# The beginning of a one-core attention and expert kernel: when the late weights are loaded, which projections TensorE makes first, and which engine rounds the first keys

## The chip, the core and the metric

The kernel runs on one core of a Trainium2 chip. A core has TensorE (PE in the profile; PEld is its weight load), VectorE (DVE), ScalarE (ACT), GpSimd (POOL) and SyncE (SP), each with a queue of its own that is worked off in order, and 16 DMA engines, to which SP and ACT give transfers here. The metric is the device time of one execution in microseconds (us), lower is better.

## What is computed

16 sequences of 512 rows of 128 numbers, in float32, go through an attention block with 16 heads of 8 columns, a layer norm, a layer of 8 experts of which each row takes 2, and another layer norm:

```python
x = _layernorm(x + _L0_attn_ref(x, Wq, bq, Wk, bk, Wv, bv, Wo, bo))     # (16, 512, 128)
# in it: scores = einsum('bhqd,bhkd->bhqk', Q, K) / sqrt(8); probs = softmax(scores)
#        intervened = probs without key 0, normalised again
#        combined = probs + 0.5 * (intervened - probs); attn_out = combined @ V, then @ Wo.T + bo
x = _layernorm(x + _L0_ffn_ref(x, gate_w, w1, w2, w3))                  # 8 experts, top 2, silu
```

## The kernel before

**Units.** The attention is cut into 64 units: a unit u is a sequence b = u // 4 and a group of 4 heads. A unit is taken through three stages in three consecutive periods. In period p the kernel makes the row maxima of unit p + 2, the scores and exponentials of unit p, and the sums over values of unit p - 1. A period has 8 steps k, and periods -2 and -1 come ahead of the first unit; they hold only maxima and preparation. `maxima(u, c)` (L632) is four bf16 matmuls into four banks `mx_ps` for the query block c of 128 rows; VectorE reduces the four banks in one instruction (L1016), and PE may write them again only then. So one block of maxima is made per two steps, and PE and DVE take turns on `mx_ps`.

**How float32 is kept.** Q and K are projected in float32 (`behind`, names q0, q1, k0, k1: query or key, first or second half of the sequence), copied to `full_q_sb`, `full_k_sb` by ACT with the bias (L855), and split into three bf16 parts. For sequence 0 DVE makes the split (`lead`, `rest`: first part, remainder, second part, remainder as third part), for the later ones POOL (`split_lead`, `split_rest`). The parts are stored to DRAM (`q_parts_d`, `k_parts_d`) and come back in the layout that the matmuls need: as operands of the maxima (`load_maxima(u)`, four loads of 64 KB: `QM`, `KM`, names `q_maxima_sb`, `k_maxima_sb`) and of the scores (`load_qk(u)`, two loads of 288 KB, `region_sb`).

**What stands at the beginning.** SP loads the first sequence's x (`xT_sb[0]`), Wk and the second x, and then, in eight issues, the weights that are not needed at once: Wv, the gate, Wo in four pieces, bv and bo. ACT loads Wq and the two biases, and waits for both biases before its first copy. PE runs 16 spare matmuls on a tile of ones, the four projections of sequence 0, and 96 more spare matmuls (`WARMING`), while the parts go to DRAM and come back. Then the periods start. In the periods -2 and -1, each block of maxima is followed by 8 spare matmuls of 512 columns (L724). The table `ONCE` says which other work stands at which step there: gc and gw fold the gate into Wv and Wo (gc waits for all eight late weights and for a halved Wo that ACT makes), v0 and v1 are the values of sequence 0, q0 to k1 with a 1 the projections of sequence 1. The projections of sequence 2 follow by the table `BEHIND`: q0 of sequence 2 at step 3 of period -1, k1 at step 3 of period 0.

**SP's queue behind that.** In this order: the stores of the first parts of sequence 0 (two for K), `load_maxima(0)` (its two Q loads are ACT's), `load_maxima(1)`, the stores of the other planes of K (three) and Q (one), `load_maxima(2)`, `load_qk(0)` and `load_qk(1)` (both wait for these stores), `load_xT(2)` (which waits until v1 of sequence 0 has been computed, since it overwrites `xT_sb[0]`), `load_qk(2)`, `load_qk(3)`, `move_negmax(0)` (the negated maxima of unit 0 as rows of the scores' operand; it waits for POOL's `split_negmax(0)`), and the stores of sequence 1.

**POOL** clears the value tiles, adds bv to the values (`values_with_bias(0)`, `values_without_key0(0)`), then splits Q of sequence 1. That split waits until the last store of Q's parts of sequence 0 has landed, as it writes the same tile.

## Time and profile before

| | us |
|---|---|
| median of 3 runs | 1178.43 (1175.75 to 1179.16) |
| the profiled execution, its own time | 1177.16 |
| its span, first to last instruction | 1175.0 |

| engine | busy us | share of the span |
|---|---|---|
| PE | 1116.9 | 95% |
| DVE | 927.2 | 79% |
| ACT | 824.8 | 70% |
| POOL | 663.2 | 56% |

The reductions of the maxima run from 17.7 to 742.7 us of the span; the experts and the last layer norm follow. The part that the change touches is the first 50 us. The granted clock of PE is 1.00 throughout. A row of the timeline gives the start in us from the span's start, the duration of the merged instructions, the engine, the line, the operation, what it writes and reads, how many there are, and in brackets the idle time ahead of it with what ended it. SPq and ACTq are the issues of DMAs on these queues: the duration is that of the issue, not of the transfer.

### The profile page before, as it was taken

The page shows a single profiled execution, that of the slowest core. Times are in us where ns is not written, and L with a number is a line of the kernel's source. Part 1 is how long each engine was busy: PE and PEld are TensorE (multiplying, and loading weights), DVE is VectorE, ACT ScalarE, POOL GpSimd, SP SyncE. Part 2 cuts the span into 40 slices and gives each one's busy share as a digit, 9 for nine tenths or more (in the row PEclk, how much of TensorE's full clock was granted, in tenths as well). Part 3 has the DMA queues.
Part 4 walks back from the last instruction along what each step waited for, and adds up shares of the span by engine and source line. Part 5 has one row for each costly group of instructions (what it writes and reads, how often), then busy time and mean ns, then how long its engine had stood idle before and what let it go on. Part 6 is the DMA issues. An engine that isn't in the chain of part 4 may idle for free. (4 is left out here: it accounts for less than half of the span.)

```text
span 1175.0 us, 23587 instructions
## 1 busy us (share of the span) xinstructions
PE 1116.9 (95%) x7236; PEld 575.7 (49%) x7240; DVE 927.2 (79%) x1421; ACT 824.8 (70%) x1668; POOL 663.2 (56%) x1003
## 2 busy tenths in 40 slices
PE   9999999999999999999999998999999999999986
PEld 6422232232222222222322222279999999999962
DVE  6888999999999999999999999855545554444435
ACT  2588888988889889888889888853544434345627
POOL 4424556666676676676676654666545433334336
PEclk9999999999999999999999999999999999999998
DMA  4453334444434343443443345353434333332247
GB/s 145 148 159 112 106 119 124 132 126 127 126 119 138 117 134 117 131 130 109 135 129 125 123 144 159 92 120 84 89 77 103 87 76 80 78 71 58 58 152 301
DMA packets 175051, 139.79 MB, mean 119 GB/s; under 512 B 89539, under 2 KB 151623, under 8 KB 174928
## 3 DMA queue, kind: packets, MB, share of 16 engines
q1 hardware_dynamic: 165672, 119.95, 36.3%
q0 software_dynamic: 8688, 18.14, 4.6%
q8 instruction: 60, 0.98, 0.4%
q14 instruction: 63, 0.52, 0.1%
q10 hardware_dynamic: 568, 0.20, 0.1%
HBM read 95.96 MB, written 42.19 MB: 118 GB/s over the span
## 5 line engine op out<-in xcount | busy, mean ns | idle before, releaser
L837 ACT ACTIVATE probs_sb<-ring_ps 128x512 f32<-128x512 f32 x1024 | 558.4, 598 | 96.9 <-PE ring_ps L643 81.1
L1016 DVE TENSOR_REDUCE rowmax_sb<-mx_ps 128x4 f32<-128x2048 f32 x256 | 586.0, 2289 | 26.3 <-PE mx_ps L632 20.7
L643 PE MATMUL ring_ps<-region_sb 74*128 74x512 bf16 x1024 | 311.4, 384 | 2.1 <-ACT probs_sb L837 2.0
L655 PE MATMUL acc_ps<-probs_sb,values_sb 128*32 128x512 f32 x2048 | 272.3, 604 | 0.0
L1690 POOL DMA_INDIRECT y_d<-probs_sb,values_sb x135 | 133.0, 985 | 190.0 <-DVE probs_sb L1329 166.0
L643 PEld LDWEIGHTS ring_ps<-region_sb 74*128 74x128 bf16 x1024 | 79.2, 97 | 312.8 <-ACT probs_sb L837 272.4
L912 ACT ACTIVATE xT_sb<-region_sb 128x512 f32 x78 | 49.2, 630 | 183.1 <-PE mx_ps L762 181.7
L1329 DVE SCALAR_TENSOR_TENSOR probs_sb<-ring_ps,values_sb 128x128 f32<-128x128 f32 x135 | 42.1, 347 | 143.2 <-issue 120.9
L1546 POOL DMA_INDIRECT rows_d<-sent_sb,pos_sb x128 | 130.1, 1016 | 41.2 <-issue 19.2
L632 PE MATMUL mx_ps<-k_maxima_sb,q_maxima_sb 32*128 32x512 bf16 x1024 | 101.0, 384 | 40.4 <-DVE rowmax_sb L1016 39.9
L783 PE MATMUL ring_ps<-region_sb,probs_sb 128*128 x1080 | 133.5, 275 | 1.6 <-DVE probs_sb L1339 1.6
L783 PEld LDWEIGHTS ring_ps<-region_sb,probs_sb 128*128 128x128 f32 x1080 | 131.0, 192 | 5.0 <-issue 2.2
L752 PE MATMUL mx_ps<-k_parts_sb,xT_sb 128*128 128x256 f32 (+1 forms) x624 | 130.5, 352 | 1.0 <-DVE k_parts_sb L1311 1.0
L1339 DVE TENSOR_TENSOR probs_sb<-mx_ps,probs_sb 128x512 f32<-128x512 f32 (+1 forms) x156 | 95.2, 619 | 25.9 <-PE mx_ps L762 18.6
L752 PEld LDWEIGHTS mx_ps<-k_parts_sb,xT_sb 128*128 128x128 f32 x624 | 106.8, 190 | 13.9 <-DVE k_parts_sb L1311 2.2
L655 PEld LDWEIGHTS acc_ps<-probs_sb,values_sb 128*32 128x32 f32 x2048 | 40.5, 108 | 97.9 <-issue 97.5
L632 PEld LDWEIGHTS mx_ps<-k_maxima_sb,q_maxima_sb 32*128 32x128 bf16 x1024 | 25.7, 90 | 111.7 <-DVE rowmax_sb L1016 102.8
L958 ACT ACTIVATE probs_sb<-mx_ps 128x1024 f32<-128x1024 f32 (+1 forms) x78 | 70.4, 903 | 4.5 <-PE mx_ps L752 4.4
L762 PE MATMUL mx_ps<-k_parts_sb,full_q_sb 128*128 128x256 f32 (+1 forms) x312 | 65.5, 353 | 0.0
L762 PE MATMUL mx_ps<-k_parts_sb,full_k_sb 128*128 128x256 f32 (+1 forms) x312 | 64.6, 350 | 0.0
L762 PEld LDWEIGHTS mx_ps<-k_parts_sb,full_q_sb 128*128 128x128 f32 x312 | 51.6, 191 | 5.3 <-issue 0.8
L1399 POOL CAST negmax_parts_sb<-negmax_sb 16x128 bf16<-16x128 f32 x64 | 17.9, 279 | 62.9 <-PE mx_ps L632 62.7
(193 smaller groups left out, 1174.6 us busy)
## 6 DMA issues: line engine op xcount, KB each, us to landing
region_sb<-q_parts_d SPq DMA_DIRECT2D x64, 288.0 KB
region_sb<-k_parts_d SPq DMA_DIRECT2D x64, 288.0 KB
k_parts_d<-k_parts_sb SPq DMA_DIRECT2D x46, 256.0 KB, 2.5
k_maxima_sb<-k_parts_d SPq DMA_DIRECT2D x128, 64.0 KB
probs_sb<-y_d SPq DMA_DIRECT2D x32, 256.0 KB, 6.9
q_maxima_sb<-q_parts_d SPq DMA_DIRECT2D x126, 64.0 KB
values_sb<-rows_d SPq DMA_DIRECT2D x57, 132.0 KB, 2.3
q_parts_d<-q_parts_sb SPq DMA_DIRECT2D x15, 384.0 KB
```

The lines of the kernel that those rows point to most:

```text
L632: last = nc.tensor.matmul(mx_ps[:, j, :], q[rows, P * c:P * (c + 1)], k[rows, :], start=True, stop=True)
L643: nc.tensor.matmul(bank, KS[b % 2][0:KR + MR, h, P * c:P * (c + 1)], QS[b % 2][0:KR + MR, h, :], start=True, stop=True).then_inc(s_ring_re ...
L655: last = nc.tensor.matmul(acc_ps[VW * j:VW * (j + 1), 0, :], VE[b % 2][:, c, HG * g + j, :], PT[u % 2][:, j, c, :], start=(c == 0), stop=( ...
L752: last = nc.tensor.matmul(up_ps[:, c, 0:n], W1T[t % 2][:, P * c:P * (c + 1)], XGT[t % 2][:, 0:n], start=True, stop=True)
L762: last = nc.tensor.matmul(lin_ps[:, c, 0:n], W3T[t % 2][:, P * c:P * (c + 1)], XGT[t % 2][:, 0:n], start=True, stop=True)
L783: last = nc.tensor.matmul(y_ps[:, at:at + D], HH[t % 2][:, c, P * w:P * (w + 1)], W2[:, bass.ds(expert + c * D, D)], start=(c == 0), stop= ...
L837: nc.scalar.activation(PT[u % 2][:, i // QC, i % QC, :], ring_bank("st", u, i), ACT.Exp, scale=SCALE).then_inc(s_ring_done, 1)
L958: nc.scalar.activation(SG[t % 2][:, :, 0:n], up_ps[:, :, 0:n], ACT.Silu).then_inc(s_silu, 1)
L1016: V.tensor_reduce(rowmax[u % 2][:, :].rearrange("p (j c) -> p j c", c=QC)[:, :, c], mx_ps[:, :, :], axis=AXX, op=ALU.max, negate=True).the ...
L1339: V.tensor_tensor(HH[t % 2][:, part, 0:n], lin_ps[:, part, 0:n], SG[t % 2][:, part, 0:n], ALU.mult)\
L1546: G.indirect_dma_start(rows_d, bass.IndirectOffsetOnAxis(ap=pos[b % 2][:, s, c:c + 1], axis=0), XE[b % 2][:, c, s, :], None).then_inc(s_sc ...
L1690: G.indirect_dma_start(y_d, bass.IndirectOffsetOnAxis(ap=XG[t % RING][:, w, D:D + 1].bitcast(i32), axis=0), YO[t % YRING][:, w, :], None, ...
```

## The change

Five things are edited: (1) PE's second block of spare matmuls has 80 instead of 96, and the 8 behind a block of maxima are 5 where the same or the next step holds an entry of `ONCE`; (2) the eight late loads stand on SP's queue behind `load_maxima(0)` instead of behind the second x; (3) `ONCE` has the projections of sequence 1 first, and gc, gw, v0, v1 after them, and POOL splits Q of sequence 1 ahead of its work on the values; (4) the first part of K of sequence 0 is rounded by ACT instead of DVE, so DVE's `lead(1)` begins with the remainder; (5) the biases have a semaphore each, so the copy of Q waits for bq alone.

```diff
-WARMING = (16, 96)
+WARMING = (16, 80)
...
-        s_biases_qk = sem("biases_qk")
+        s_biases_qk = [sem(f"bias_{n}") for n in "qk"]
+        s_first_cast = sem("first_keys_cast")
...
-        ONCE = {(-2, 1): ("gc", 0), (-2, 2): ("gw", 0), (-2, 3): ("v0", 0), (-2, 4): ("v1", 0), (-2, 5): ("q0", 1),
-                (-2, 6): ("q1", 1), (-2, 7): ("k0", 1), (-1, 0): ("k1", 1)}
+        ONCE = {(-2, 1): ("q0", 1), (-2, 2): ("q1", 1), (-2, 3): ("k0", 1), (-2, 4): ("k1", 1), (-2, 5): ("gc", 0),
+                (-2, 6): ("gw", 0), (-2, 7): ("v0", 0), (-1, 0): ("v1", 0)}
...
             load_xT(1)
-            for dst, src in ((wvg_sb[:, 0:D], wvT), (gate_sb[:, :], gateT)):
-                sp.dma_start(dst, src).then_inc(s_weights, 16)
...
-            sp.dma_start(bo_sb[:, :], bo.to_broadcast([P, D])).then_inc(s_weights, 16)
...
-            sp.wait_ge(s_first_split, 4)
+            sp.wait_ge(s_first_cast, 1)
             sp.dma_start(by_head(k_parts_d[0, 2:3]), qk_parts[1][:, 0:1, :]).then_inc(s_first_stored[1], 16)
-            sp.wait_ge(s_first_split, 6)
+            sp.wait_ge(s_first_split, 5)
             sp.dma_start(by_head(k_parts_d[0, 0:2]), qk_parts[1][:, 0:2, :]).then_inc(s_first_stored[1], 16)
             load_maxima(0)
+            for dst, src in ((wvg_sb[:, 0:D], wvT), (gate_sb[:, :], gateT)):
+                sp.dma_start(dst, src).then_inc(s_weights, 16)
...
+            sp.dma_start(bo_sb[:, :], bo.to_broadcast([P, D])).then_inc(s_weights, 16)
             load_maxima(1)
...
-                            for n in range(8):
+                            for n in range(5 if {(p, k), (p, k + 1)} & ONCE.keys() else 8):
                                 nc.tensor.matmul(acc_ps[:, 0, :], QM[p + 2][:, 0:P], KM[p + 2][:, :], start=True, stop=True)
...
-            act.wait_ge(s_biases_qk, 16 * 2)
...
+                    elif name[1] == "0":
+                        act.wait_ge(s_biases_qk[which], 16)
...
             for what in BEFORE:
                 behind(*what)
+            act.wait_ge(s_ring_done, ring_at["k1", 0] + 1)
+            nc.scalar.activation(qk_parts[1][:, 0, :], full[1][:, :], ACT.Copy).then_inc(s_first_cast, 1)
             act.wait_ge(*first_stored(0))
...
-                dve.wait_ge(s_ring_done, ring_at[("q1", "k1")[which], 0] + 1)
-                V.tensor_copy(parts[:, 0, :], exact[:, :]).then_inc(s_first_split, 1)
-                dve.wait_ge(s_first_split, n + 1)
+                if which == 0:
+                    dve.wait_ge(s_ring_done, ring_at["q1", 0] + 1)
+                    V.tensor_copy(parts[:, 0, :], exact[:, :]).then_inc(s_first_split, 1)
+                    dve.wait_ge(s_first_split, 1)
+                else:
+                    dve.wait_ge(s_first_cast, 1)
...
             clear(1)
+            split_lead(1, 0)
+            split_rest(1, 0)
             values_with_bias(0)
             values_without_key0(0)
-            split_lead(1, 0)
-            split_rest(1, 0)
             beside_reduction(-1, 1)
```

**PE, from the spare matmuls to the second block of unit 1, before.** `mx_ps` is written by a block of maxima, `acc_ps` by spare matmuls; `wq_sb`, `wk_sb` mark projections, `centre_sb` to `bo_sb` gc, `ysum_sb` gw, `wv_gate_sb,xT_sb` the values.

```order
L714 MATMUL acc_ps<-ones_sb 128x256 x96
L632 MATMUL mx_ps<-k_maxima_sb,q_maxima_sb 128x512 x4
L724 MATMUL acc_ps<-k_maxima_sb,q_maxima_sb 128x512 x8
L679 MATMUL ring_ps<-gate_sb,centre_sb 128x8
L680 MATMUL ring_ps<-ident_sb,wo_half_gate_sb 128x128
L681 MATMUL ring_ps<-ident_sb,bo_sb 128x128
L632 MATMUL mx_ps<-k_maxima_sb,q_maxima_sb 128x512 x4
L724 MATMUL acc_ps<-k_maxima_sb,q_maxima_sb 128x512 x8
L685 MATMUL ring_ps<-wv_gate_sb,ysum_sb 128x8 x2
L690 MATMUL ring_ps<-wv_gate_sb,xT_sb 128x136 x2
```

The same stretch of PE now, to gc and the block of maxima behind it:

```order
L715 MATMUL acc_ps<-ones_sb 128x256 x80
L633 MATMUL mx_ps<-k_maxima_sb,q_maxima_sb 128x512 x4
L725 MATMUL acc_ps<-k_maxima_sb,q_maxima_sb 128x512 x5
L674 MATMUL ring_ps<-xT_sb,wq_sb 128x256
L633 MATMUL mx_ps<-k_maxima_sb,q_maxima_sb 128x512 x4
...
L725 MATMUL acc_ps<-k_maxima_sb,q_maxima_sb 128x512 x5
L674 MATMUL ring_ps<-xT_sb,wk_sb 128x256
L680 MATMUL ring_ps<-gate_sb,centre_sb 128x8
L681 MATMUL ring_ps<-ident_sb,wo_half_gate_sb 128x128
L682 MATMUL ring_ps<-ident_sb,bo_sb 128x128
L633 MATMUL mx_ps<-k_maxima_sb,q_maxima_sb 128x512 x4
```

The group gc has moved from behind the first block of maxima to behind the third, where it follows the last projection of sequence 1; v1 now stands behind the first block of unit 1, in period -1.

**SP, from the second x on, now** (before, the rows of `wvT` to `bo` stood directly behind the second `xT`, ahead of the stores):

```order
L419 DMA xT_sb<-xT 128x512
L488 DMA q_parts_d<-q_parts_sb 128x2x512
L490 DMA k_parts_d<-k_parts_sb 128x512
L492 DMA k_parts_d<-k_parts_sb 128x2x512
L457 DMA k_maxima_sb<-k_parts_d 64x1x512 x2
L495 DMA wv_gate_sb<-wvT 128x128
L495 DMA gate_sb<-gateT 128x8
L497 DMA wo_sb<-woT 32x1x128 x4
L499 DMA bv_sb<-bv 128x128
L500 DMA bo_sb<-bo 128x128
L456 DMA q_maxima_sb<-q_parts_d 64x1x512
L457 DMA k_maxima_sb<-k_parts_d 64x1x512
```

The eight issues now stand ahead of `load_maxima(1)` and of all that follows it: the other stores, `load_maxima(2)`, `load_qk(0)`, `load_qk(1)` and `load_xT(2)`, whose order among themselves is as before.

## Rows read from the trace of the kernel before

**Rows 1.** The line L1016 alone: duration ns min/median/max, first and last start.

```profile
L1016 DVE TENSOR_REDUCE rowmax_sb<-mx_ps x256: 2256/2293/2296, 17.7 to 742.7; 128x4 f32<-128x2048 f32 x128
```

**Rows 2.** The timeline, start of the kernel to the first maxima.

```profile
5.58 0.84 ACT L855 ACTIVATE full_q_sb<-ring_ps,bq_sb 128x256 f32<-128x256 f32 x2 [1.86 <-DMA bk_sb<-bk]
6.36 0.95 ACT L855 ACTIVATE full_k_sb<-ring_ps,bk_sb 128x256 f32<-128x256 f32 x2
6.64 10.64 PE L714 MATMUL acc_ps<-ones_sb 128*128 128x256 bf16 x96
7.98 0.42 DVE L992 CAST k_parts_sb<-full_k_sb 128x512 bf16<-128x512 f32 x1
9.61 0.37 SPq L498 DMA_DIRECT2D k_parts_d<-k_parts_sb  x1
11.83 1.15 SPq L463 DMA_DIRECT2D k_maxima_sb<-k_parts_d  x2
17.21 0.10 PEld L632 LDWEIGHTS mx_ps<-k_maxima_sb,q_maxima_sb 32*128 32x128 bf16 x4 [0.21 <-issue]
```

**Rows 3.** The page: a group by line, with busy us, mean ns, idle before.

```profile
L912 ACT ACTIVATE xT_sb<-region_sb 128x512 f32 x78 | 49.2, 630 | 183.1 <-PE mx_ps L762 181.7
```

**Rows 4.** Busy time by stretch: PE, PEld, DVE, ACT, POOL, PEclk, DMA share, GB/s.

```profile
11.50:15.50 4.00, 4.00 (x39) 3.57 (x38) 3.47 (x1) 0.31 (x1) 3.78 (x5) 1.00 0.25 73
23.00:35.00 12.00, 11.67 (x68) 5.75 (x67) 9.17 (x4) 3.23 (x10) 7.55 (x11) 1.00 0.76 213
```

**Rows 5.** The timeline: reductions of the maxima, second, fifth and sixth block.

```profile
20.46 2.29 DVE L1016 TENSOR_REDUCE rowmax_sb<-mx_ps 128x4 f32<-128x2048 f32 x1 [0.51 <-PE mx_ps L632]
29.61 2.29 DVE L1016 TENSOR_REDUCE rowmax_sb<-mx_ps 128x4 f32<-128x2048 f32 x1 [0.73 <-PE mx_ps L632]
32.41 2.29 DVE L1016 TENSOR_REDUCE rowmax_sb<-mx_ps 128x4 f32<-128x2048 f32 x1 [0.51 <-PE mx_ps L632]
```

**Rows 6.** The timeline: gc and its halved Wo; one cycle of period -1.

```profile
12.00 0.31 ACT L849 ACTIVATE wo_half_gate_sb<-wo_sb 128x128 f32<-128x128 f32 x1 [4.69 <-issue]
19.07 0.41 PEld L679 LDWEIGHTS ring_ps<-gate_sb,centre_sb 128*128 128x128 f32 x2
19.56 0.27 PE L681 MATMUL ring_ps<-ident_sb,bo_sb 128*128 128x128 f32 x1
31.95 0.10 PEld L632 LDWEIGHTS mx_ps<-k_maxima_sb,q_maxima_sb 32*128 32x128 bf16 x4 [0.42 <-DVE rowmax_sb L1016]
32.29 1.90 PE L724 MATMUL acc_ps<-k_maxima_sb,q_maxima_sb 128*128 128x512 bf16 x8
33.81 0.41 PEld L673 LDWEIGHTS ring_ps<-xT_sb,wq_sb 128*128 128x128 f32 x2
34.66 0.47 ACT L855 ACTIVATE full_q_sb<-ring_ps,bq_sb 128x256 f32<-128x256 f32 x1 [2.18 <-PE ring_ps L673]
34.75 0.10 PEld L632 LDWEIGHTS mx_ps<-k_maxima_sb,q_maxima_sb 32*128 32x128 bf16 x4 [0.54 <-DVE rowmax_sb L1016]
```

**Rows 7.** The timeline: issues on SP's queue.

```profile
2.18 0.43 SPq L424 DMA_DIRECT2D wv_gate_sb<-wvT  x1
6.56 0.43 SPq L429 DMA_DIRECT2D bo_sb<-bo  x1
16.71 0.45 SPq L506 DMA_DIRECT2D q_parts_d<-q_parts_sb  x1
21.46 0.81 SPq L475 DMA_DIRECT2D region_sb<-q_parts_d  x1
25.80 0.34 SPq L418 DMA_DIRECT2D xT_sb<-xT  x1
```

**Rows 8.** Issues of one DMA each: count, KB, us from issue to landing.

```profile
q_parts_d<-q_parts_sb SPq DMA_DIRECT2D x1, 256.0 KB, 2.2
xT_sb<-xT SPq DMA_DIRECT2D x1, 256.0 KB, 5.6
```

**Rows 9.** The timeline: PE's first spare matmuls.

```profile
1.06 3.60 PE L710 MATMUL acc_ps<-ones_sb 128*128 128x256 bf16 x16 [1.06 <-POOL ones_sb L1371]
```

More of the change, by code:

```diff
@@ L380, in split_done @@
         def split_done(b, which):
-            return (s_first_split, 8 - which) if b == 0 else (s_split, split_no(b, which) + 1)
+            return (s_first_split, 7 - which) if b == 0 else (s_split, split_no(b, which) + 1)
         def halves(t):
@@ L422, in _ @@
             load_xT(1)
-            for dst, src in ((wvg_sb[:, 0:D], wvT), (gate_sb[:, :], gateT)):
-                sp.dma_start(dst, src).then_inc(s_weights, 16)
-            for j in range(HG):
-                sp.dma_start(wo_sb[VW * j:VW * (j + 1), :],
-                             woT.rearrange("(g j d) n -> j g d n", j=HG, d=DK)[j]).then_inc(s_weights, 16)
-            sp.dma_start(bv_sb[:, :], bv.to_broadcast([P, D])).then_inc(s_weights, 16)
-            sp.dma_start(bo_sb[:, :], bo.to_broadcast([P, D])).then_inc(s_weights, 16)
             def by_head(planes):
@@ L494, in _ @@
             sp.dma_start(by_head(q_parts_d[0, 0:2]), qk_parts[0][:, 0:2, :]).then_inc(s_first_stored[0], 16)
-            sp.wait_ge(s_first_split, 4)
+            sp.wait_ge(s_first_cast, 1)
             sp.dma_start(by_head(k_parts_d[0, 2:3]), qk_parts[1][:, 0:1, :]).then_inc(s_first_stored[1], 16)
-            sp.wait_ge(s_first_split, 6)
+            sp.wait_ge(s_first_split, 5)
             sp.dma_start(by_head(k_parts_d[0, 0:2]), qk_parts[1][:, 0:2, :]).then_inc(s_first_stored[1], 16)
             load_maxima(0)
+            for dst, src in ((wvg_sb[:, 0:D], wvT), (gate_sb[:, :], gateT)):
+                sp.dma_start(dst, src).then_inc(s_weights, 16)
+            for j in range(HG):
+                sp.dma_start(wo_sb[VW * j:VW * (j + 1), :],
+                             woT.rearrange("(g j d) n -> j g d n", j=HG, d=DK)[j]).then_inc(s_weights, 16)
+            sp.dma_start(bv_sb[:, :], bv.to_broadcast([P, D])).then_inc(s_weights, 16)
+            sp.dma_start(bo_sb[:, :], bo.to_broadcast([P, D])).then_inc(s_weights, 16)
             load_maxima(1)
@@ L821, in _ @@
             nc.scalar.dma_start(wq_sb[:, :], wqT).then_inc(s_weights_qk, 16)
-            for dst, src in ((bq_sb, bq), (bk_sb, bk)):
-                nc.scalar.dma_start(dst[:, :], src).then_inc(s_biases_qk, 16)
+            for which, (dst, src) in enumerate(((bq_sb, bq), (bk_sb, bk))):
+                nc.scalar.dma_start(dst[:, :], src).then_inc(s_biases_qk[which], 16)
             act.wait_ge(s_pool_const, 1)
             nc.scalar.activation(warm[:, :], ones[:, 0:1], ACT.Identity).then_inc(s_warm, 1)
-            act.wait_ge(s_biases_qk, 16 * 2)
             def ring_bank(*what):
@@ L988, in lead @@
             def lead(which):
-                exact, parts, n = full[which], qk_parts[which], 3 * which
-                dve.wait_ge(s_ring_done, ring_at[("q1", "k1")[which], 0] + 1)
-                V.tensor_copy(parts[:, 0, :], exact[:, :]).then_inc(s_first_split, 1)
-                dve.wait_ge(s_first_split, n + 1)
+                exact, parts, n = full[which], qk_parts[which], 2 * which
+                if which == 0:
[4 more added lines that the diff above has]
+                    dve.wait_ge(s_first_cast, 1)
                 V.tensor_tensor(exact[:, :], exact[:, :], parts[:, 0, :], ALU.subtract).then_inc(s_first_split, 1)
@@ L1000, in rest @@
                 exact, parts = full[which], qk_parts[which]
-                dve.wait_ge(s_first_split, 6 + (which == 0))
+                dve.wait_ge(s_first_split, 5 + (which == 0))
                 V.tensor_tensor(parts[:, 2, :], exact[:, :], parts[:, 1, :], ALU.subtract).then_inc(s_first_split, 1)
```

## The prediction

> **What bounds the kernel now.** I read the line of the reductions first. 256 of them start between 17.7 and 742.7 us [rows 1], so one comes every 2.84 us while it lasts 2.29 us, and the rest is PE writing the four banks again. The alternation of PE and DVE on `mx_ps` sets the pace from the first block of maxima until 742.7 us. The work behind that waits for it. So what counts is when this chain starts and how long its first cycles are: a us that the change takes from the first eight blocks comes off the end, unless something later in the beginning waits for another thing. The timeline shows when the chain starts: PE runs its 96 spare matmuls from 6.64 us, and the first weight load of the maxima at 17.21 follows with 0.21 us of plain issue, waiting for no transfer [rows 2]. The spare matmuls, not the operands, release the first block. Then come SP's queue and the state of the DMA engines, since three of the five edits touch them [rows 4, 7, 8].
>
> **The first block: bound by the spare matmuls, then by the operands.** 96 spare matmuls take 10.64 us, 0.111 us each [rows 2]. Sixteen fewer take 1.77 us off. They start behind the fourth projection. The split bias semaphores let ACT begin a little before 5.58, where it waited for bk [rows 2], but PE has the first projection ready only just before that, so this is worth under 0.1 us; I take 0.05. PE would be ready at 17.21 - 1.77 - 0.05 = 15.4.
>
> The operands may be later. DVE no longer rounds K, 0.42 us [rows 2]. ACT does it in about 0.63 us, the mean of its 128 x 512 copies [rows 3], behind its last projection copy, which ends at 6.36 + 0.95 = 7.31 [rows 2], so by 8.0 us, when DVE is still ending Q and would have taken K (7.98). It is hidden, barely: half a us more on ACT would cost what DVE saves. K's second store goes at 9.2 instead of 9.61, and the first K load at 11.4 instead of 11.83 [rows 2]. Four loads of 64 KB, 262 KB, move at 73 GB/s between 11.5 and 15.5 [rows 4]: 3.6 us, to 15.1, and the last completion some tenths later. I take 15.8 for the operands now. The bounds are 15.4 (PE itself) and 16.8 (they landed before 17.21 last time, and come 0.4 earlier). **First block 15.8 instead of 17.21: -1.4 us, between -1.8 and -0.4.**
>
> **The cycles of period -2.** From the second to the fifth reduction three cycles take 29.61 - 20.46 = 9.15 us, 3.05 each; the next, where PE has less, takes 2.80 [rows 5], which is the reduction and the refill. Eight spare matmuls take 1.90 us [rows 6], so three fewer give PE 0.7 us back, more than the 0.25 it was late. That would save 3 x 0.25 = 0.75 us.
>
> But the new place of gc brings a wait. gc needs the halved Wo, which ACT makes, in order, behind its copy of the last projection of sequence 1. That projection now stands right ahead of gc on PE. From the start T of the third block: with 8 spare matmuls a projection's weights load at T + 1.86 (31.95 to 33.81) and its copy ends at T + 3.2 (34.66 + 0.47) [rows 6]; with 5 that is T + 1.2 and T + 2.5. Then 0.31 for the halved Wo [rows 6], T + 2.9 with the hand-overs, then gc itself, 0.76 from 19.07 to 19.83 [rows 6]: the next block starts at about T + 3.5, not T + 2.8. **+0.7 us, between 0 and +0.9** (behind PE's wait stand the fourth block and the DVE that reduces it). The late weights themselves are no cause: issued by 17.3 they land at about 20, and gc is at 24.
>
> The blocks then start at 15.8, 18.6, 21.4, 24.9 and 27.7, the last being unit 1's first, which stood 2.8 before the 31.95 of [rows 6], at 29.16. **Up to here the change gains 1.45 us.**
>
> **What SP's queue costs.** The eight late issues run from 2.18 to 6.99 [rows 7], 4.8 us, under nothing that waits. Now they stand behind `load_maxima(0)`, so all behind them is issued 4.8 - 0.4 = 4.4 us later. `load_maxima(1)` and `load_maxima(2)` have slack of more than that. The chain through the stores has less. The store of Q's last plane goes at 21.1 instead of 16.71; `load_qk(0)` waited for it until 21.46 [rows 7], 4.75 us, where a store on idle queues lands in 2.2 us [rows 8]. So `load_qk(0)` starts between 23.8 (SP's own issues end there) and 25.9 (the same 4.75). I take 24.4, because the loads ahead of the store no longer queue behind `load_maxima(0)`, which saves about 1.5 us of the 4.75.
>
> What the trace shows of that queueing: while loads of maxima run, a quarter of the DMA engines' time is busy and 73 GB/s move; with `load_qk` it is 0.76 and 213 GB/s [rows 4]. The Trainium skill, page "DMA: Bandwidth & Descriptors", section "Why a DMA increments its semaphore by 16 and not by 1", says that such a transfer is spread over the largest number up to 16 that divides both outer sizes, always the lowest engines, which gives four here: the trace agrees (0.25). By that rule every store has its share behind these four, and SP's wait would keep most of its 4.75 us; if transfers spread evenly it would fall to 2.2.
>
> `load_xT(2)` was issued at 25.80 and took 5.6 us, to 31.4 [rows 7, 8], 10.0 us behind the start of `load_qk(0)`: 1.18 MB of `load_qk` and its own 0.26 MB at 213 GB/s [rows 4] are 6.8 us, the rest is first byte and completion. Now it lands at 24.4 + 10.0 = 34.4. It can't be issued before v1 is computed, at about 29.8, so 29.8 + 2.2 = 32.0 is the floor, and 25.9 + 10.0 = 35.9 the ceiling. PE wants it for q0 of sequence 2, 1.86 us after the second block of unit 1 starts: before at 33.81 [rows 6], 2.4 us after it had landed; now at 27.7 + 2.8 + 1.86 = 32.4. **PE waits about 2.0 us** (0 to 3.5), and behind it stand the blocks of maxima, for whose reduction DVE waits. The third block of unit 1 starts about 0.65 us after q0 can: 35.1, against 34.75 before [rows 6]. **The 1.45 us are gone and 0.35 is lost.** That is max(33.3, 35.1), so whatever the first block gained or gc cost is hidden under it.
>
> Further on, `load_qk(2)` and `(3)`, the maxima rows of unit 0 and the stores of sequence 1 pass through the same DMA engines, which are now full 3 us longer. I give that +0.05, up to +0.7. POOL's new order makes its split of Q wait for the late store, but it would otherwise wait for v1; it ends its work for unit 0 at about the same time. Nothing.
>
> **Sum.** 1177.16 + 0.35 + 0.05 = 1177.6 on the profiled execution. This lies 1.27 below the median of the three runs, 1178.43, to which I refer the forecast: **1178.8 us**. By the two ends of the wait for x it is 1178.43 - 1.4 = 1177.0 and 1178.43 + 2.5 = 1180.9.
>
> **Rivals.**
> *The transfer is in time.* If the four slow DMA engines are less full than I think, x is there at 32.4 and only the 1.45 us (1.85 if PE bounds the first block, 2.15 if gc waits for nothing as well) count: 1176.3 to 1177.0. For it: the late weights leave the queues empty when `load_maxima(1)` comes. Against: the floor of 23.8 for SP's own issues plus the 6.8 us of bytes already passes 32.
> *The wait cools PE.* The granted clock reads 1.00 all along, but the first 16 spare matmuls stand 0.225 us apart (3.60 us) [rows 9] and the later ones 0.111 [rows 2]: the pace of 1.2 and of 2.4 GHz. If 2 to 3.5 us without a matmul bring the slower pace back, 8 spare matmuls take 3.8 instead of 1.9 us and a cycle 4.7 instead of 2.8. The slow stretch at the start lasted 3.6 us, so one or two cycles: 1.9 to 3.8 us on top, 1180.7 to 1182.6, likely 1181.0. It decides from a wait above about 2 us. The Trainium skill, "TensorE: Matmul & The Clock Gate", "Why this matters for your kernels", warns of such gaps between bursts; no stretch of these rows has one.
> *The first operands are late.* If the loads for unit 0 land at 16.8, the first block gains 0.4 only; the sum stays 1178.8, as the wait for x covers it.
>
> **Chances.** Forecast 0.52, transfer in time 0.25, cooled PE 0.15, late first operands 0.08. The likeliest time is the forecast's. For 8 in 10 the range goes from 1175.8, which takes in the first rival and the spread of the runs, to 1181.8, most of the second. The bound of 0.3% (3.5 us) is about what a measurement of this kernel tells from no change. Almost every case lies inside: faster by over 0.3% has 0.05 (first rival and a low set of runs), slower 0.07 (second rival's upper half), within it 0.88.
>
> **What would show it.** In the profile after: the first weight load of the maxima at 15.8; reductions 2.8 apart in period -2 but for one cycle of 3.5 with gc; the issue of `load_qk(0)` near 24.4; a wait of PE's projection of sequence 2 on the DMA of `xT_sb`, of about 2 us, at 32.4; the block behind it near 35.1; the last reduction at about 743. The forecast is wrong in its mechanism if q0 of sequence 2 waits for nothing, and in its size if the cycles behind that wait are longer than 2.8.

## The result and the profile after

| | us |
|---|---|
| kernel before, median of 22 runs | 1176.62 (1174.71 to 1179.16) |
| changed kernel, median of 22 runs | 1178.84 (1176.18 to 1182.2, and one run of 1369.05) |
| ratio, 95% interval | 1.0020 (1.0013 to 1.0027) |
| profiled execution of the changed kernel | 1179.02, span 1177.3 |

The run of 1369.05 us had a mean granted clock of 0.752; it counts in the median, which is 1178.66 without it, and not in the ratio.

The change costs 1.5 to 3.2 us, below the 0.3% that the prediction took as no difference. The median is where the forecast put it, but the shift isn't: more runs of the kernel before brought its median down from the 1178.43 of three runs to 1176.62, so the forecast of +0.4 stands against a measured +2.2.

The line of the reductions after, as [rows 1]:

```profile
L1023 DVE TENSOR_REDUCE rowmax_sb<-mx_ps x256: 2254/2293/2296, 17.5 to 746.6; 128x4 f32<-128x2048 f32 x128
```

The last reduction was at 742.7 and is at 746.6. All of this difference arises within the first 42 us; from there the two traces run 3.8 to 3.9 us apart.

The spans differ by less, because the rest behind the last reduction, 432.2 us before, is 430.7 after. This doesn't look like scatter: the profiles of the twelve kernels of this case fall into groups. The rest is 432.2 and 433.3 us in the two kernels with all the spare matmuls (before and e4), 431.5 in e2, which has 14 elsewhere, 430.9 in e10, which keeps the 8 behind each block, and 429.7 to 430.7 in the eight others. The difference arises between 370 and 390 us behind the last reduction, in the experts' part. Busy time of that stretch (columns as in [rows 4]) for before, e4, the changed kernel and e8:

```profile
1112.74:1132.74 20.00, 17.33 (x134) 15.11 (x134) 6.68 (x20) 7.24 (x13) 6.62 (x7) 1.00 0.22 44
1116.48:1136.48 20.00, 17.23 (x133) 15.07 (x134) 6.80 (x20) 7.13 (x13) 6.56 (x7) 1.00 0.22 43
1116.57:1136.57 20.00, 19.67 (x153) 16.77 (x152) 7.80 (x22) 7.13 (x13) 6.87 (x7) 1.00 0.20 40
1111.43:1131.43 20.00, 19.67 (x147) 16.25 (x146) 6.88 (x20) 7.13 (x13) 6.66 (x7) 1.00 0.22 43
```

PE is busy for 17.3 of the 20 us in the first two and for 19.7 in the others. In this stretch VectorE waits 4.9 us for loads of `values_sb` in the kernel before, 3.2 in e4, 0.7 in e8 and not at all in the changed kernel. Why spare matmuls at the beginning of the kernel should matter there is not shown; no experiment was made on it. The times bear it out: by the last reductions the changed kernel would be 3.8 us slower than the one before and e8 1.3 us faster, and the medians say 2.2 slower and 2.9 faster. So the last reduction tells what the beginning costs, and the rest has to be told apart from it.

**The start.** The timeline of the changed kernel, which answers to [rows 2]:

```profile
4.56 2.05 PE L674 MATMUL ring_ps<-xT_sb,wq_sb 128*128 128x256 f32 x4
7.40 8.90 PE L715 MATMUL acc_ps<-ones_sb 128*128 128x256 bf16 x80
8.10 0.63 ACT L920 ACTIVATE k_parts_sb<-full_k_sb 128x512 bf16<-128x512 f32 x1
9.95 0.37 SPq L492 DMA_DIRECT2D k_parts_d<-k_parts_sb  x1
12.18 1.39 SPq L457 DMA_DIRECT2D k_maxima_sb<-k_parts_d  x2
17.02 0.39 PE L633 MATMUL mx_ps<-k_maxima_sb,q_maxima_sb 32*128 32x512 bf16 x4 [0.73 <-DMA k_maxima_sb<-k_parts_d]
```

80 spare matmuls end at 16.30, but the operands land at 16.98: now the transfer releases the first block, at 17.02 instead of 17.21. In this execution the first projections ran at a slower pace than in the profile before (four matmuls 2.05 us; 1.44 there), so the whole beginning stood 0.3 to 0.8 us later than there. That comes and goes from one execution to the next: in the profiles of the experiments below that keep 80 spares, the first reduction is at 15.9 to 17.6.

**Period -2 and gc.** The timeline:

```profile
20.27 2.29 DVE L1023 TENSOR_REDUCE rowmax_sb<-mx_ps 128x4 f32<-128x2048 f32 x1 [0.50 <-PE mx_ps L633]
23.06 2.29 DVE L1023 TENSOR_REDUCE rowmax_sb<-mx_ps 128x4 f32<-128x2048 f32 x1 [0.50 <-PE mx_ps L633]
25.48 0.36 PE L680 MATMUL ring_ps<-gate_sb,centre_sb 128*128 128x8 f32 x2 [0.85 <-ACT wo_half_gate_sb L849]
26.49 2.29 DVE L1023 TENSOR_REDUCE rowmax_sb<-mx_ps 128x4 f32<-128x2048 f32 x1 [1.14 <-PE mx_ps L633]
29.29 2.29 DVE L1023 TENSOR_REDUCE rowmax_sb<-mx_ps 128x4 f32<-128x2048 f32 x1 [0.50 <-PE mx_ps L633]
```

Cycles of 2.8 us instead of the 3.05 of [rows 5], and one of 3.43, where gc waits 0.85 us for the halved Wo.

**SP, x and the clock.** The timeline from SP's last store of sequence 0 on, with PE, which answers to [rows 6] and [rows 7]:

```profile
22.06 0.45 SPq L507 DMA_DIRECT2D q_parts_d<-q_parts_sb  x1
26.41 0.80 SPq L469 DMA_DIRECT2D region_sb<-q_parts_d  x1
30.92 0.34 SPq L419 DMA_DIRECT2D xT_sb<-xT  x1
36.66 0.67 PE L674 MATMUL ring_ps<-xT_sb,wq_sb 128*128 128x256 f32 x2 [2.79 <-DMA xT_sb<-xT]
37.26 0.54 PE L633 MATMUL mx_ps<-k_maxima_sb,q_maxima_sb 32*128 32x512 bf16 x4
37.73 3.40 PE L725 MATMUL acc_ps<-k_maxima_sb,q_maxima_sb 128*128 128x512 bf16 x8
41.94 2.29 DVE L1023 TENSOR_REDUCE rowmax_sb<-mx_ps 128x4 f32<-128x2048 f32 x1 [1.81 <-PE mx_ps L633]
```

`load_qk(0)` waits for the store until 26.41 (before 21.46). The third x is issued at 30.92, when v1 is there, and lands at 36.52, and PE stands still for 2.79 us. The eight spares behind the next block then take 3.40 us instead of 1.90, and the block after that comes 4.10 us behind it instead of 2.80. The view by stretch has the reason (columns as in [rows 4]; the last three are the granted clock, DMA share and GB/s):

```profile
34.00:38.00 4.00, 1.34 (x7) 0.53 (x8) 0.54 (x2) 0.47 (x1) 3.69 (x6) 0.92 0.85 241
38.00:40.00 2.00, 2.00 (x6) 0.73 (x5) 2.00 (x1) 0.00 (x0) 0.31 (x1) 0.50 0.87 239
40.00:42.00 2.00, 2.00 (x11) 0.80 (x9) 0.19 (x2) 0.41 (x1) 0.00 (x0) 0.80 0.98 317
42.00:46.00 4.00, 3.86 (x24) 2.02 (x23) 3.42 (x2) 1.45 (x4) 1.16 (x2) 1.00 0.38 131
```

From 38 to 40 us the clock is 0.50, the 1.2 GHz level, and it is back at 1.00 by 42. Before, it is 1.00 in each of these stretches. So the 3.9 us come in two steps: reduction 6 (counted from 0) is at 37.84 instead of 35.20, which is 2.64, and reduction 7 at 41.94 instead of 38.00, which is 1.30 more.

This is not one odd execution. Each run has a mean granted clock over its span, which falls with the time at the slow level, and in the changed kernel it goes with the time. (The clock isn't 1.00 throughout in any kernel, the one before included: the record also reads 0.50 for the last 7 to 10 us of each profile, behind PE's last matmul, where it costs nothing. That is why the highest mean is 0.998.)

| mean clock | changed kernel: runs, median us | kernel before: runs, median us |
|---|---|---|
| 0.998 | none | 10, 1177.4 |
| 0.997 | 2, 1177.0 | 17, 1177.0 |
| 0.996 | 10, 1178.0 | 1, 1178.0 |
| 0.995 | 5, 1180.0 | 2, 1178.0 |
| 0.994 | 4, 1181.2 | none |

The runs of before are the 30 of the first set of experiments; the changed kernel's are its 22 without the one of 1369.05 us. The profiled execution has a mean of 0.996. Nine runs have less and are longer than most; where their clock fell once more, no trace shows.

### The profile page after: what moved, and what is told of

It is laid out like the page before. It is cut to its first block, busy times and chain, and to the rows that moved or that the text cites. A ratio compares the mean times of both kernels' runs of the same rounds, so it can differ in the third digit from the quotient of the medians.

```text
span 1177.3 us, 23530 instructions
## 1 busy us (share of the span) xinstructions
PE 1115.3 (95%) x7209; PEld 574.0 (49%) x7209; DVE 926.8 (79%) x1420; ACT 825.7 (70%) x1669; POOL 664.4 (56%) x1003
## 4 chain that ended last, share of the span: by engine, by line
PE 49%; DVE 39%; issue 9%; DMA 2%; ACT 1%; SPq 0%; POOL 0%; ACTq 0%; DVEq 0%; POOLq 0%
DVE rowmax_sb L1023 32%; PE ring_ps L784 10%; PE mx_ps L753 10%; PE mx_ps L763 10%; PE ring_ps L644 5%; PE acc_ps L656 5%; PE mx_ps L633 3%; DVE TN_sb L1032 3%; PE mx_ps L815 1%; PE ring_ps L691 1%; DVE stats_sb L1055 1%; PE ring_ps L815 1%; DVE meanvar_sb L1062 1%; PE ring_ps L699 1%; PE acc_ps L725 0%
```

## Experiments

Reductions are counted from 0, so reduction 7 is the eighth, and reduction 12 belongs to the first block of unit 3. All times are medians beside the kernel before on the same chip: e1 to e4 against 1177.35, e5 to e8 against 1176.36, e9 and e10 against 1175.70. In the diffs + is what the experiment has.

The theory: the late weights on SP's queue make the third x late (2.6 us), and the wait cools PE (1.3 us). The rivals: the new order of the projections is the cause; or what is lost is the gain of the spare matmuls alone.

### e1: the late weights back in their old place

```diff
 (changed kernel)
             load_xT(1)
+            the eight loads of wvT ... bo
...
             load_maxima(0)
-            the eight loads of wvT ... bo
```

> The changed kernel with one part undone: the eight late loads stand on SP's queue behind the second x again. Theory (they hold up the store of Q's last plane, so load_qk and the third x): load_qk(0) goes near 21 us instead of 26.4, the third x is issued right behind v1 (about 30) and lands by 32.5, PE waits for it less than 0.5 us or not at all, and no block of spare matmuls takes over 2 us; the eighth reduction starts near 37 instead of 41.9, and the time is 4 to 5 us below the changed kernel, so 1 to 2.5 us below the kernel before. Rival (the wait comes from the new order of the projections or from fewer spare matmuls): the eighth reduction stays near 42 and the time near that of the changed kernel.

1178.04 us, ratio 1.0009 (0.9998 to 1.0020). The first half of the expectation held: `load_qk(0)` is issued at 21.24, the x lands at 33.38 and PE hardly waits; reduction 7 is at 37.37, 0.6 us ahead of before. The x is issued at 30.62, only 0.3 us earlier than in the changed kernel, since it waits for v1 in both. It lands after 2.77 us instead of 5.60, because the transfers of `load_qk` were issued 5.2 us earlier. (That it is their bytes that hold the x is read from the times: it took 2.7 to 2.8 us in e1, e3 and e4, issued 3 to 6 us behind the last issue of `load_qk(1)`, and 5.6 us before and in the changed kernel, issued 1.1 to 1.3 us behind it.) The time didn't follow: 4 to 5 us below the changed kernel were expected, and 0.8 came. The last reduction is at 744.66, 1.9 us behind before. The gain is lost at a second place. The timeline of e1, then the stretches:

```profile
30.62 0.34 SPq L419 DMA_DIRECT2D xT_sb<-xT  x1
38.03 1.64 SPq L450 DMA_DIRECT2D k_parts_d<-k_parts_sb  x3
52.30 0.40 PE L633 MATMUL mx_ps<-k_maxima_sb,q_maxima_sb 32*128 32x512 bf16 x4 [1.86 <-DMA k_maxima_sb<-k_parts_d]
53.70 1.94 PE L656 MATMUL acc_ps<-probs_sb,values_sb 128*32 128x512 f32 x8
57.52 1.06 PE L656 MATMUL acc_ps<-probs_sb,values_sb 128*32 128x512 f32 x8
```

```profile
52.00:53.00 1.00, 0.65 (x6) 0.29 (x7) 0.19 (x1) 0.00 (x0) 0.00 (x0) 1.00 0.69 250
53.00:54.00 1.00, 1.00 (x7) 0.26 (x9) 1.00 (x1) 0.84 (x2) 0.00 (x0) 0.60 0.27 80
54.00:56.00 2.00, 2.00 (x10) 0.12 (x2) 1.10 (x1) 0.74 (x2) 0.00 (x0) 0.50 0.27 92
```

The operands of unit 3 land at 52.16 (before 50.33). PE waits 1.86 us, its clock falls to 0.50 again, and eight matmuls of one kind take 1.94 us there and 1.06 later. So the weights are a cause of the first wait, and not the only one of the loss.

### e2: 14 spare matmuls in PE's wait for x

```diff
 (changed kernel, ahead of the projection q0 of sequence 2)
+                    if (p, k) == (-1, 3):
+                        for n in range(14):
+                            nc.tensor.matmul(acc_ps[:, 0, :], QM[1][:, 0:P], KM[1][:, :], start=True, stop=True)
```

> The changed kernel with 14 more spare matmuls of 512 columns (3.0 us at 0.216 each) on PE right ahead of q0 of sequence 2, where it waited 2.8 us for the third x. Theory (the wait costs twice, by itself and by the slower pace of PE behind it): the wait stays, x lands near 36.5 as before, but the eight spare matmuls behind it take 1.9 instead of 3.4 us and the eighth reduction comes 1.0 to 1.5 us earlier; the time is 1 to 1.5 us below the changed kernel. Rival (the 3.4 us have another cause, such as traffic of operands): they stay at 3.4 us, and the time is the same or up to 0.3 us longer.

1179.78 us, ratio 1.0023 (1.0011 to 1.0035). The stretches of e2 beside those of the changed kernel above:

```profile
38.00:40.00 2.00, 2.00 (x13) 0.97 (x10) 1.70 (x1) 0.43 (x1) 0.31 (x1) 1.00 0.88 238
40.00:42.00 2.00, 1.70 (x11) 0.71 (x11) 1.50 (x2) 0.47 (x1) 0.00 (x0) 1.00 0.94 276
```

The clock stays at 1.00 and reductions 6 and 7 are 2.79 apart instead of 4.10 (reduction 6 itself is at 38.30 instead of 37.84, as x lands 0.6 us later in this execution: PE still waits 0.36 us for it behind the 14). That the pause lowers the clock is thereby shown. The 1 to 1.5 us that were expected of it did not come: reduction 11 is at 52.36, but 12 comes only at 56.16, for PE now waits for the operands of unit 3:

```profile
55.64 0.40 PE L633 MATMUL mx_ps<-k_maxima_sb,q_maxima_sb 32*128 32x512 bf16 x4 [1.49 <-DMA k_maxima_sb<-k_parts_d]
```

The last reduction is at 746.73, that of the changed kernel at 746.57. The second bound lies right behind the first. Behind this wait of 1.49 us the clock stayed at 1.00.

### e3: the late loads on ACT's queue

```diff
 (changed kernel)
             load_maxima(0)
-            the eight loads of wvT ... bo, by sp
...
                 nc.scalar.dma_start(maxima_rows(QM, 0, r), maxima_queries(0)).then_inc(maxima_in(0)[0], 16)
+            the same eight, by nc.scalar
```

> The changed kernel with the eight late loads issued by ScalarE, behind its two Q loads of unit 0, instead of by SP. They are then neither ahead of the first unit's operands nor on SP's queue. Theory: SP's stores go 4.7 us earlier, load_qk(0) near 21.5, no wait for the third x; ACT issues until about 17.5, when it has its first projection copy to make near 19, so it pays nothing; the time is like e1, within 0.5 us. Rival (what matters is the traffic behind the first operands, whoever issues it): the wait for the third x stays above 1 us.

1177.16 us, ratio 1.0001 (0.9992 to 1.0011), some 2 us below the changed kernel. `load_qk(0)` goes at 21.96 and x lands at 32.27, with the weights issued nearly as late as in the changed kernel (11.8 to 17.7 us; 13.6 to 18.3 there). So the first wait comes from the eight issues on SP's queue, and not from the traffic of the weights behind the first operands. The second stall is as in e1: 2.1 us at unit 3's operands, clock 0.50 to 0.51 from 53 to 56, last reduction 744.36.

### e4: 96 and 8 spare matmuls again

```diff
 (changed kernel)
-WARMING = (16, 80)
+WARMING = (16, 96)
...
-                            for n in range(5 if {(p, k), (p, k + 1)} & ONCE.keys() else 8):
+                            for n in range(8):
```

> The changed kernel with the numbers of spare matmuls of the kernel before: 96 in the second block and 8 behind every block of maxima of period -2. Theory (all that fewer spare matmuls gain lies ahead of the wait for the third x and is lost in it): the first block comes no more than 1 us later, the wait for x becomes shorter by as much, the eighth reduction stays within 0.7 us of the changed kernel's and the time within 0.7 us. Rival (fewer spare matmuls cool PE, and that is what costs): the slow block of eight behind the wait (3.4 us) is gone, and the time is 1.5 us or more below the changed kernel.

1181.47 us (7 runs), ratio 1.0036 (1.0019 to 1.0052). The first reduction is at 18.40, and the wait for x shrinks to 0.65 us, with the clock at 1.00; reduction 7 is at 40.44, earlier than the changed kernel's 41.94. Yet reduction 12 is at 55.97 and the last at 746.48, as in the changed kernel and e2. In e4 and e2 it is unit 3's operands that set this (PE waits 1.95 and 1.49 us for them), in the changed kernel the first wait and the slow stretch (56.06). Up to the last reduction the number of spares counts for nothing, as expected. The time was expected within 0.7 us of the changed kernel, and by the ratios it lies 1.9 us higher, with overlapping intervals. The profile has that difference behind the last reduction: 433.3 us instead of 430.7, as told with the result.

### e5 and e6: the new order undone, with the weights early and late

e5 is the kernel before plus edits 1, 4 and 5; e6 has edit 2 as well.

```diff
 (e6: changed kernel; e5: e1)
-        ONCE = {(-2, 1): ("q0", 1), (-2, 2): ("q1", 1), (-2, 3): ("k0", 1), (-2, 4): ("k1", 1), (-2, 5): ("gc", 0),
-                (-2, 6): ("gw", 0), (-2, 7): ("v0", 0), (-1, 0): ("v1", 0)}
+        ONCE = {(-2, 1): ("gc", 0), (-2, 2): ("gw", 0), (-2, 3): ("v0", 0), (-2, 4): ("v1", 0), (-2, 5): ("q0", 1),
+                (-2, 6): ("q1", 1), (-2, 7): ("k0", 1), (-1, 0): ("k1", 1)}
...
-            split_lead(1, 0)
-            split_rest(1, 0)
             values_with_bias(0)
             values_without_key0(0)
+            split_lead(1, 0)
+            split_rest(1, 0)
```

> The kernel before with three parts of the change alone: fewer spare matmuls (80, and 5 in period -2), the biases with a semaphore each, and K's first part by ScalarE. Late weights and the order of the projections are as before. Theory (these three gain, the two moves cost: the late weights by the store of Q's last plane, the order by v1, on which the third x waits, and by the loads behind it): no wait for the third x, none for the operands of unit 3, the reductions of unit 3 start 1 to 1.5 us ahead of the kernel before, time 1.0 to 1.5 us below it. Rival (the operands of unit 3 arrive when they arrive, whatever the first block does): they arrive as before, near 50.3, so a gain of the first block above 1.2 us is lost there, and the time is within 0.3 us of the kernel before or above it.

> The changed kernel with the order of ONCE and of POOL as before, so gc stands behind the first block while its weights are still loaded behind the first operands. Theory: gc waits for the weights, which land about 20.8, so the second block comes near 21.6 instead of 20.3 (+1.3 us); load_qk(0) goes near 26.4 as in the changed kernel; v1 is ready by 28, so the third x is issued right behind load_qk(1) at 29.7, lands near 36 and PE waits 1 to 2.5 us for it. The time is within 1.5 us of the changed kernel, 1.5 to 4 us above the kernel before. Rival (the new order alone is what costs): within 0.7 us of the kernel before.

e5: 1173.49 us, ratio 0.9977 (0.9967 to 0.9987): faster than both kernels. Its profile is of the slowest of its nine runs (1175.88; the others 1172.69 to 1174.06), and it shows what was expected to be gone, a wait for unit 3's operands and a slow stretch behind it:

```profile
51.38 0.40 PE L633 MATMUL mx_ps<-k_maxima_sb,q_maxima_sb 32*128 32x512 bf16 x4 [1.54 <-DMA k_maxima_sb<-k_parts_d]
53.00:54.00 1.00, 1.00 (x8) 0.00 (x0) 1.00 (x1) 0.78 (x2) 0.00 (x0) 0.50 0.27 93
54.00:56.00 2.00, 2.00 (x12) 0.51 (x9) 0.66 (x2) 0.74 (x2) 0.28 (x1) 0.50 0.11 38
```

So the second bound is near in the old order too. The operands land at 51.24 here and at 48.72 in e8, whose order and weights are the same. With the new order and the first wait mended (e1, e3, e9) they land at 51.7 to 52.2.

e6: 1178.03 us, ratio 1.0020 (1.0010 to 1.0029). In e6 gc stands behind the first block and waits for the weights. `load_qk(0)` goes at 25.27, and PE doesn't wait for the third x, as had been expected (1 to 2.5 us), because it comes there some 3 us later itself. Its timeline and stretches:

```profile
20.50 0.36 PE L680 MATMUL ring_ps<-gate_sb,centre_sb 128*128 128x8 f32 x2 [3.45 <-ACT wo_half_gate_sb L849]
21.55 2.29 DVE L1023 TENSOR_REDUCE rowmax_sb<-mx_ps 128x4 f32<-128x2048 f32 x1 [3.34 <-PE mx_ps L633]
26.11 2.29 DVE L1023 TENSOR_REDUCE rowmax_sb<-mx_ps 128x4 f32<-128x2048 f32 x1 [2.27 <-PE mx_ps L633]
```

```profile
20.00:24.00 4.00, 3.50 (x16) 1.90 (x17) 2.29 (x1) 0.76 (x3) 0.00 (x0) 0.66 0.51 171
24.00:28.00 4.00, 4.00 (x15) 2.21 (x16) 1.89 (x1) 0.70 (x4) 0.00 (x0) 0.50 0.40 142
```

With its first reduction at 15.91 it is at 29.55 with the fourth, 3.0 behind before; its last reduction is at 745.36. Again a wait of PE and then the lower clock. With the other edits in place the table is:

| | old order | new order |
|---|---|---|
| weights early | e5 0.9977 | e1 1.0009 |
| weights late (SP) | e6 1.0020 | changed kernel 1.0020 |

Each of the edits 2 and 3 alone spends the gain of the spares and more: edit 3 costs 3.8 us (e1 less e5), edit 2 costs 5.1 (e6 less e5). Together they cost no more than edit 2 alone. The order also decides by which way edit 2 costs: gc's wait for the weights themselves in the old order, SP's queue and the third x in the new one.

### e7: the stores of the other planes ahead of `load_maxima(1)`

```diff
 (e5)
             load_maxima(0)
+            the four stores of the other planes
             load_maxima(1)
-            the four stores of the other planes
```

> The three parts of e5, and on SP's queue the stores of the other planes of sequence 0 ahead of the loads for the maxima of unit 1 instead of behind them. Theory (a store lands late because its share on the DMA engines of the maxima's loads stands behind them): the stores land 2.2 to 3 us after issue instead of up to 4.9, load_qk(0) goes near 18 instead of 21.4, load_qk for all four units and the maxima rows of unit 0 end 1 to 2 us earlier, the operands of unit 3 arrive earlier by what POOL allows (up to 1 us), and the time is the same as e5 or up to 0.5 us below. Rival (queueing is not what delays these stores): they still take over 4 us, and nothing moves.

1173.77 us, ratio 0.9975 (0.9966 to 0.9984), as e5. Issued from 13.20 on, ahead of these loads, the four stores land 2.2, 2.3, 3.6 and 3.5 us after their issue. With the loads ahead of them it is 2.2, 2.2, 5.4 and about 5.3 in the profile of e5, but 2.2, 2.2, 4.0 and 3.8 in that of e8, whose SP queue has the same order. So the loads cost the last two stores between 0.4 and 1.8 us, and the first two nothing; what makes the last two land later than the first two even in e7 is not shown. The rival of the expectation (over 4 us, nothing moves) is out, and the 2.2 to 3 us of the theory hold for two of the four. It doesn't help, because SP then has eight issues of maxima loads ahead of `load_qk(0)`, which goes at 19.69, and nothing waits for it.

### e8 and e10: fewer spare matmuls and nothing else

```diff
 (kernel before; e10 has the first of the two only)
-WARMING = (16, 96)
+WARMING = (16, 80)
...
-                            for n in range(8):
+                            for n in range(5 if {(p, k), (p, k + 1)} & ONCE.keys() else 8):
```

> The kernel before with one part of the change alone: 80 spare matmuls in the second block, and 5 instead of 8 in period -2. Theory: the first block starts when its operands have landed, near 16.2 instead of 17.2 (-1.0 us), three cycles of period -2 take 2.8 instead of 3.05 (-0.75 us), and of the 1.75 us at least 1.0 reach the end, the rest being lost where the operands of unit 3 arrive. Time 0.7 to 1.7 us below the kernel before. Rival (the spare matmuls keep PE at the fast pace and are worth their time): matmuls behind them stand at the slower pace, and the time is the same or above.

> The kernel before with 80 instead of 96 spare matmuls in the second block, and nothing else: half of e8. Theory: the first block starts near 16.8 (-0.8 us), three cycles of period -2 stay at 3.05, so the last reduction is 0.75 us behind e8's, and the time between that of e8 and the kernel before: 0.7 to 2.2 us below it. Rival (the 5 instead of 8 give nothing, since these cycles wait for something else): the same time as e8 within 0.3 us and cycles of 2.8 us.

e8: 1173.49 us, ratio 0.9975 (0.9965 to 0.9984), the fastest here with e5. e10: 1175.29, ratio 0.9990 (0.9979 to 1.0001). Reductions of e8, then of e10, by the timeline:

```profile
17.28 2.29 DVE L1016 TENSOR_REDUCE rowmax_sb<-mx_ps 128x4 f32<-128x2048 f32 x1 [1.24 <-PE mx_ps L632]
20.08 2.29 DVE L1016 TENSOR_REDUCE rowmax_sb<-mx_ps 128x4 f32<-128x2048 f32 x1 [0.50 <-PE mx_ps L632]
...
31.26 2.29 DVE L1016 TENSOR_REDUCE rowmax_sb<-mx_ps 128x4 f32<-128x2048 f32 x1 [0.50 <-PE mx_ps L632]
```

```profile
19.68 2.29 DVE L1016 TENSOR_REDUCE rowmax_sb<-mx_ps 128x4 f32<-128x2048 f32 x1 [0.50 <-PE mx_ps L632]
22.75 2.29 DVE L1016 TENSOR_REDUCE rowmax_sb<-mx_ps 128x4 f32<-128x2048 f32 x1 [0.78 <-PE mx_ps L632]
```

In e8 every cycle is 2.80; from the first to the sixth reduction it takes 13.98 us, before 32.41 - 17.66 = 14.75. In e10 the three cycles behind the first are still 3.03 to 3.07. By the ratios (0.10% and 0.25%) the 2.9 us of e8 would be 1.2 for the 16 and the rest for the three fewer behind each block, but the interval of e10 reaches up to no gain. By the profiles the beginning of e8 gives less than its time: the last reduction is at 741.4, 1.3 us ahead of before, and the rest behind it is 430.3 us instead of 432.2. e8 equals e5, so the split bias semaphores and ScalarE's rounding bring nothing measurable.

### e9: the third x behind `load_qk(2)`

```diff
 (e1)
-            load_xT(2)
-            for u in (2, 3):
-                load_qk(u)
+            load_qk(2)
+            load_xT(2)
+            load_qk(3)
```

> e1 (the changed kernel, late weights at their old place) with one swap on SP's queue: load_qk(2) goes ahead of load_xT(2) instead of behind it, so SP's wait for v1, now 5 us later than in the kernel before, no longer holds that transfer. Theory (in e1 this wait delays load_qk(2), load_qk(3), the stores of sequence 1 and through them the operands of unit 3, which came at 52.2): load_qk(2) goes near 24.5, the stores of K of sequence 1 land by 41.8 instead of 43.0, the operands of unit 3 by 51, the gap between the reductions at the start of period 1 falls from 4.2 to 3.3 us or less and the slow one behind it (4.1) is gone; time 1.5 to 2.5 us below e1. Rival (the operands of unit 3 are late in e1 for their own traffic, not for the wait): they stay at 52, and the time is that of e1.

1175.92 us, ratio 0.9997 (0.9987 to 1.0008). In e1 the x, which waits for v1 under the new order, holds both `load_qk` and all that follows. Here one goes ahead, and the timeline shows:

```profile
35.39 0.67 PE L674 MATMUL ring_ps<-xT_sb,wq_sb 128*128 128x256 f32 x2 [1.04 <-DMA xT_sb<-xT]
38.84 1.64 SPq L450 DMA_DIRECT2D k_parts_d<-k_parts_sb  x3
53.36 2.29 DVE L1023 TENSOR_REDUCE rowmax_sb<-mx_ps 128x4 f32<-128x2048 f32 x1 [0.57 <-PE mx_ps L633]
56.16 2.29 DVE L1023 TENSOR_REDUCE rowmax_sb<-mx_ps 128x4 f32<-128x2048 f32 x1 [0.50 <-PE mx_ps L633]
```

The last of K's stores lands at 42.52 although it was issued 0.8 us later (e1 43.03), and at unit 3 there is no wait and no slow stretch. But this is hardly the work of the swap. Unit 3's operands land at 51.77, only 0.4 us earlier than in e1 (52.16) and later than the 51 expected, while PE comes to unit 3 1.9 us later (reduction 11 at 50.50 instead of 48.63) and so has nothing left to wait for. What makes it later is a wait of 1.04 us for x, with the clock at 1.00, and a slow stretch at the start: PE waits 1.97 us for the first operands, and the clock is 0.50 for most of the time from 18 to 22. The last reduction is at 743.87, 0.8 ahead of e1, and the intervals of e1 and e9 overlap. So whether SP's wait for v1 is what delays unit 3's operands stays open.

## Why the prediction was right in the median and short in the shift

- **First block, 15.8 forecast.** The profile has 17.02, 0.2 outside the bounds (15.4 to 16.8). The price of a spare matmul was right (80 in 8.90 us), and that the operands would take over was right. Missed was that the start itself moves from one execution to another; 15.5 and 17.1 both occur. On PE the term stayed hidden, as the prediction said, but SP's queue started late by it as well (next point but one).
- **Cycles of period -2 and gc.** 2.8 and one of 3.43 where 2.8 and 3.5 were forecast: right. From the first to the fifth reduction 11.82 us, forecast 11.9.
- **The store and `load_qk(0)`: the step that failed.** Forecast 24.4 within 23.8 to 25.9, measured 26.41, outside. The 2.0 us have two parts. The store was issued at 22.06 instead of 21.1, since SP's K loads went at 12.18 and not at the 11.4 of the forecast. And it took 4.33 us where the prediction had let the 4.75 us shrink by 1.5, to 3.25, since the loads ahead of it would no longer queue behind others. The change doesn't remove the 64 KB loads right ahead of the store, which cost it 0.4 to 1.8 us by e7. The Trainium skill, "DMA: Bandwidth & Descriptors", section "Why a DMA increments its semaphore by 16 and not by 1", has the rule for how many DMA engines a transfer is spread over. The prediction worked out from it that the wait would keep most of its length, which came true here, though the first two stores, which land in 2.2 us behind the same loads, don't fit that working. The row of the store in [rows 7] already had the length, and the prediction chose against both.
- **From there to x.** 10.0 us forecast, 10.1 measured (26.41 to 36.52). PE's wait 2.0 forecast (0 to 3.5), 2.79 measured. The block behind it 35.1 forecast, 37.26 measured. The 2 us of `load_qk(0)` are all there.
- **The cooled PE**, given 0.15, is what happened: clock 0.50, one cycle of 4.10 instead of 2.80. The size that was priced for it, 1.9 us for a cycle, was 1.3. It should have had more weight: with its own range for the wait reaching 3.5 us, the condition (a wait above about 2 us) was met at the forecast's own value, and waits of 1.54 and 1.86 us were enough in e5 and e1, though 1.95 in e4 was not. The Trainium skill, "TensorE: Matmul & The Clock Gate", "Why this matters for your kernels", warns of gaps between bursts of matmuls; the trace of the changed kernel agrees, with the clock at 0.50 behind a gap of 2.79 us.
- **"Further on +0.05, up to +0.7."** Here a second bound was overlooked: the operands of unit 3. In the changed kernel it costs nothing because the first wait is longer, but it is what a repair of the first meets (e1, e2, e3, e4). Edit 3 brings it nearer: by it v1 and so the third x are late and SP's queue stands behind them, and the operands of unit 3 land at 51.7 to 52.2 in e1, e3 and e9 and at 48.5 to 49.8 in e7, e8 and e10. That edit 3 costs 3.8 us is shown; that it does so through SP's queue is argued (see e9). And the e5 profile has the same stall without edit 3, so the bound was near already.
- **POOL's order.** Nothing was forecast. Its split of Q waits 7.99 us for the late store, and the stores of K of sequence 1, for which it makes the parts, are issued at 38.34 instead of 37.58. No wait of PE in the changed kernel goes back to it; the 0.8 us would count only where unit 3's operands are the bound.
- **"The work behind that waits for it."** It does, but it didn't keep its length: the rest behind the last reduction is 1.5 us shorter than before. No term of the prediction stands for that.
- **The sum.** Forecast +0.4 on the profiled execution, last reduction near 743; measured +1.9, and 746.6. So the chain of the maxima lost some 3.5 us more than forecast (2.2 by the later x, 1.3 by the clock), and the shorter rest hid 1.5 of them. That the median came out at 1178.84 is luck in both: the high reference of three runs (1178.43) made up for the 1.8 us of cost that remained missing.

## What to carry to other kernels

Count each issue that is put ahead on a queue, and then the queue's first wait for a transfer: eight loads that nobody was waiting for cost 2.2 us on SP's queue in front of a store (the changed kernel less e3), and nothing measurable on ACT's (e3 against e1). When a gain at the head of a chain is lost, look for the next transfer with little slack before repairing the first: two waits in a row give back only their difference. Build the edits one at a time: here the simplest alone (fewer spare matmuls) was worth 2.9 us, and the edits 2 and 3 spent it. And look at the whole trace of each: 1.3 of the 2.9 us were gained where the edit was made, and the rest in a part of the kernel that nobody had touched. A single profile can also be of an odd run, as that of e5 is; its place among the run's times tells.

## What the runs showed of the hardware

- In the first 60 us of the twelve profiles, PE's clock fell to 0.50 shortly after waits of 1.54 us (e5), 1.86 (e1), 1.97 (e9, for the first operands), 2.06 (e3), 2.79 (changed kernel) and 3.45 (e6). It stayed at 1.00 after 1.49 (e2), 1.78 (e7, for the first operands) and 1.95 (e4, for unit 3's operands), and after all shorter waits; in the experts' part it stayed there after 2.18 (e4). So between 1.5 and 2.2 us the length of the wait alone doesn't decide. The fall doesn't come in the wait but 0.7 to 1.5 us into the work behind it, and it came over the work on scores and values (e1) as over spare matmuls.
- At the start the column of the granted clock reads 1.00 while the first spare matmuls stand 0.225 us apart [rows 9]; the pace of the instructions tells more than the column there. How long this lasts differs from one execution to the next.
- Of the four 128 KB stores behind the 64 KB loads, the first two landed in 2.2 us (2.7 in e3) and the last two in 3.8 to 5.4; with the loads behind them (e7) it was 2.2 and 3.5 to 3.6. The transfer of x took 5.6 us issued 1.1 to 1.3 us behind `load_qk(1)` (before, changed kernel), and 2.7 to 2.8 issued 3 to 6 us behind (e1, e3, e4).
